# Seven stored left operands for the second token half, on a fused low-bit linear and gated MLP

## What is computed

```python
# x: (8, 256, 1024) f32; D = 1024, F = 2752
w   = dequantised(codebook, weight + 0.5 * lora_B @ lora_A) + 0.5 * lora_B @ lora_A
x1  = x + x @ w.T
g   = x1 @ W_gate.T + 0.5 * (x1 @ A_gate[i].T) @ B_gate[i].T     # i: adapter of the sample
u   = x1 @ W_up.T   + 0.5 * (x1 @ A_up[i].T)   @ B_up[i].T
a   = silu(g) * u
out = x1 + a @ W_down.T + 0.5 * (a @ A_down[i].T) @ B_down[i].T
```

## Time and profile before

| | us |
|---|---|
| median of 3 runs | 1620.17 (1619.71 to 1621.79) |
| the profiled execution's own time | 1620.05 |
| its span, first to last instruction | 1618.4 |
| TensorE busy in it | 1572.8 |
| VectorE busy | 1235.7 |
| ScalarE busy | 568.4 |
| GpSimd busy | 534.3 |
| mean granted TensorE clock | 0.993 |

### The profile page before, as it was taken

One profiled execution on the slowest core, in us unless ns is written; L12 is line 12 of the kernel. 1 busy time (PEld: TensorE's weight loads), 2 busy tenths in 40 slices (PEclk: granted clock), 3 DMA queues, 4 the chain that ended last, 5 costly groups with the idle time before them and its releaser, 6 DMA issues.

```text
span 1618.4 us, 21109 instructions
## 1 busy us (share of the span) xinstructions
PE 1572.8 (97%) x6968; PEld 1293.7 (80%) x6968; DVE 1235.7 (76%) x1575; ACT 568.4 (35%) x1006; POOL 534.3 (33%) x401
## 2 busy tenths in 40 slices
PE   6999999989999999996999999999999999999999
PEld 4888887868888878875888888888888888888887
DVE  6998969878888889987776888878675576785443
ACT  5411135433333333353433333333343233233231
POOL 4320013645555455653444555555410000000000
PEclk9999999999999999998999999999999999999999
DMA  9551174767887898881335666665267677586463
GB/s 287 126 115 64 63 227 107 194 176 218 213 217 196 218 234 221 238 309 51 99 122 137 175 182 180 183 179 155 83 198 209 163 184 191 148 222 206 157 188 119
DMA packets 368460, 281.25 MB, mean 174 GB/s; under 512 B 225120, under 2 KB 266848, under 8 KB 368224
## 3 DMA queue, kind: packets, MB, share of 16 engines
q1 hardware_dynamic: 284800, 245.11, 53.1%
q10 hardware_dynamic: 81472, 28.99, 7.1%
q0 software_dynamic: 2080, 5.80, 1.8%
HBM read 166.27 MB, written 110.85 MB: 171 GB/s over the span
## 4 chain that ended last, share of the span: by engine, by line
PE 81%; DVE 9%; SPq 3%; DMA 3%; issue 2%; ACT 1%; POOL 1%; DVEq 0%; ACTq 0%; POOLq 0%
PE bank L1826 18%; PE bankA L1826 12%; PE bankC L1826 12%; PE bank L2062 9%; PE bankC L2062 6%; PE bankA L2062 6%; PE bankT L1971 3%; PE bank L1971 3%; PE bankT L2062 3%; DVE xl L1337 2%; PE bankT L1877 1%; PE bankT L1878 1%; DVE rl L1328 1%; PE bankC L1842 1%; DMA WT_d<-wt 1%
## 5 line engine op out<-in xcount | busy, mean ns | idle before, releaser
L1023 ACT CAST rh<-wt 128x512 fp32r<-128x512 f32 x253 | 156.2, 620 | 363.9 <-PE bankC L1842 79.1
L1328 DVE TENSOR_TENSOR rl<-wt,rh 128x512 fp32r<-128x512 f32 x253 | 233.7, 931 | 21.7 <-ACT rh L1023 21.5
L1496 DVE TENSOR_TENSOR opl<-opl,oph 128x512 fp32r<-128x512 f32 (+1 forms) x154 | 107.6, 700 | 155.7 <-ACT oph L1139 155.4
L1826 PE MATMUL bank<-xh,rh 128*128 128x512 f32 x528 | 206.3, 391 | 3.1 <-issue 3.1
L1826 PE MATMUL bank<-xl,rh 128*128 128x512 f32 x528 | 206.0, 390 | 0.0
L1826 PE MATMUL bank<-xh,rl 128*128 128x512 f32 x528 | 206.0, 390 | 0.0
L1139 ACT CAST oph<-opl 128x512 fp32r<-128x512 f32 (+1 forms) x154 | 95.6, 621 | 268.4 <-DMA opl<-LT_d 260.5
L1826 PE MATMUL bankC<-xh,rh 128*128 128x512 f32 x352 | 138.8, 394 | 3.2 <-DVE xl L1337 1.9
L1826 PE MATMUL bankC<-xl,rh 128*128 128x512 f32 x352 | 138.5, 393 | 0.0
L1826 PE MATMUL bankC<-xh,rl 128*128 128x512 f32 x352 | 138.3, 393 | 0.0
L1826 PE MATMUL bankA<-xl,rh 128*128 128x512 f32 x352 | 137.1, 389 | 0.0
(11 more groups left out here) (209 smaller groups left out, 3664.9 us busy)
## 6 DMA issues: line engine op xcount, KB each, us to landing
opl<-LT_d SPq DMA_DIRECT2D x148, 256.0 KB, 2.9
WT_d<-wt SPq DMA_DIRECT2D x88, 256.0 KB, 3.2
RT_d<-dt SPq DMA_DIRECT2D x70, 256.0 KB, 3.2
opl<-RT_d SPq DMA_DIRECT2D x70, 256.0 KB, 3.8
LT_d<-ev ACTq DMA_DIRECT2D x60, 256.0 KB, 2.7
wb<-WT_d SPq DMA_DIRECT2D x44, 256.0 KB, 3.3
wt<-WT_d SPq DMA_DIRECT2D x44, 256.0 KB, 4.0
dn<-in_L_cond_W_down_dram SPq DMA_DIRECT2D x86, 128.0 KB, 3.9
```

The lines of the kernel that those rows point to most:

```text
L1023: nc.scalar.copy(rh[:, v % RING, 0:KH * rows], wsrc(mm, RSRC[p])).then_inc(s_hi, 1)
L1328: dv.tensor_tensor(rl[:, v % RING, 0:KH * rows], wsrc(mm, RSRC[p]), rh[:, v % RING, 0:KH * rows].bitcast(f32), ALU.subtract).then_inc(s_lo, 1)
L1496: dv.tensor_tensor(opl[0:rows, L_AT[n % NL], :], opl[0:rows, L_AT[n % NL], :].bitcast(f32), oph[0:rows, L_AT[n % NL], :].bitcast(f32), ALU ...
L1826: last = te.matmul(OUT[p], a[:, u % RING, cols], b[:, OPND[p], k, :], start=k == 0 and n == 0, stop=k == KH - 1 and n == 2 and (p in (0, 1 ...
```

## The change

- The first pass stores all seven forms of each block, once they are made (`store_form`, `FT_d`, 256 KB each), not the four quarters. The second pass loads them in pairs of 512 KB (`load_forms`, 77 loads) into ten slots `wq`, which lie over `wn` and `wt`, and GpSimd makes no weight sums in it.
- `w_s3` no longer waits for a store. `w_tr(mm, 0)` waits until five forms of the block before have landed (`s_fa`), `w_tr(mm, 3)` for the seventh, `w_s4` for the raw L12.
- The adapter rows A are summed once (`a_sums`, four GpSimd instructions) and patched into the seven forms of blocks 0 and 1 in 14 stores, spread over blocks 7 to 10.
- `act_sum` 3 writes `s1a` and not `ev`, so VectorE's `take` of an up block waits for the sum and not for its store. The sums, the down-adapter products `td` and their splits have other slots, above all in the two blocks after a change of row-group kind (`it` = 1, 12) and of pass (`it` = 11).
- `load_bn` and `load_an` move from SyncE's queue to ScalarE's. At the start, lora_A is SyncE's first load; lora_B and the first half of x come first on ScalarE's; VectorE splits lora_A ahead of the codebook arithmetic.

The forms, their stores and their loads:

```diff
-    WT_d = dram("WT_d", [2 * NJ, 4, P, KD // 2 * P], f32)
+    FT_d = dram("FT_d", [2 * NJ * 7, P, KD // 2 * P], f32)
-        wb = place("wb", [P, 4, KH * P], f32, S0 + 20480)
+        NQ = 10
+        wq = place("wq", [P, NQ, KH * P], f32, S0 + 20480)
+        def form(v):
+            return wt[:, RSRC[v % 7], :] if v < 7 * NH else wq[:, (v - 7 * NH) % NQ, :]
+        def form_ready(eng, v):
+            if v < 7 * NH:
+                s, n = ((s_tr, 1), (s_sum, 2), (s_tr, 4), (s_sum, 3), (s_sum, 1), (s_tr, 3), (s_sum, 4))[v % 7]
+                eng.wait_ge(s, 4 * (v // 7) + n)
             else:
+                pair = (v - 7 * NH) // 2
+                eng.wait_ge(s_wl[pair % len(s_wl)], 16 * (pair // len(s_wl) + 1))
...
+                def store_form(v):
+                    form_ready(sp, v)
+                    sp.dma_start(FT_d[v, :, :], form(v)).then_inc({2: s_f12, 6: s_f4}.get(v % 7, s_fa), 16)
+                def load_forms(pair):
+                    v = 2 * pair
+                    if pair == 0:
+                        sp.wait_ge(s_wal, 16 * 14)
                         sp.wait_ge(s_tr, 4 * NH)
...
+                    if pair == 2:
+                        sp.wait_ge(s_sum, 4 * NH)
+                        sp.wait_ge(s_fa, 80 * NH)
+                        sp.wait_ge(s_f12, 16 * NH)
+                        sp.wait_ge(s_f4, 16 * NH)
+                    if pair >= 2:
+                        sp.wait_ge(s_lo, 7 * NH + (-3, 0, -2)[pair - 2] if pair < 5 else 7 * NH + 2 * (pair - len(s_wl)) + 2)
+                    sp.dma_start(wq[:, v % NQ:v % NQ + 2, :], FT_d[v:v + 2, :, :].rearrange("k p n -> p k n")).then_inc(s_wl[pair % len(s_wl)], 16)
...
-                    if p in (1, 2, 3, 4) and mm + 1 < NH:
-                        store_wt(mm + 1, p - 1)
+                    if p == 1 and mm < NH:
+                        store_form(7 * mm + 6)
+                    for n in {1: (0,), 3: (5,), 4: (2, 4), 5: (1, 3)}.get(p, ()):
+                        if mm + 1 < NH:
+                            store_form(7 * (mm + 1) + n)
...
-                    if p == 5 and NH <= mm + 2 < NM:
-                        load_wt(mm + 2)
+                    for pair in range(7 * NH // 2):
+                        if u == 7 * NH + ((-11, -9, -6, -4, -6)[pair] if pair < 5 else 2 * pair - 11):
+                            load_forms(pair)
```

On GpSimd:

```diff
                     else:
-                        gp.wait_ge(s_al, 4 * it + 3)
-                        ins = tt(a12, a11, a12, ALU.subtract)
+                        gp.wait_ge(s_sst[0], 16 * (it + 1))
+                        ins = tt(s1a[r, :], a11, a12, ALU.subtract)
...
-                    turn = (5, 5, 7, 9) if first(it - 1) else (1, 1, 3, 7) if it == NJ else (1, 1, 3, 5)
-                    if p == 0 and 0 <= mm < NM:
+                    turn = (5, 5, 7, 7) if first(it - 1) else (4, 4, 6, 6) if it == NJ else (1, 1, 3, 4)
+                    if p == 0 and mm < NH:
                         w_s4(mm)
...
-                    if p == 2 and 0 <= mm + 1 < NM:
+                    if p == 2 and mm + 1 < NH:
                         w_s12(mm + 1)
```

On ScalarE:

```diff
+                    if (m, p) == (1, 6) and it != NJ - 1 and it + 2 < NIT:
+                        load_bn(it + 2)
+                    if (m, p) == (1, 6) and it != NJ - 1 and it + 1 < NIT:
+                        load_an(it + 1)
```

On VectorE:

```diff
-                    if n in (0, 2):
-                        wait(dve, s_wst[n], 16 * mm)
+                    if n == 0:
+                        wait(dve, s_fa, 80 * mm)
+                    if n == 3:
+                        wait(dve, s_f4, 16 * mm)
...
                         if m == 1:
                             wait(dve, s_a11, 16 * it)
-                            wait(dve, s_sst[3], 16 * it)
+                            wait(dve, s_as, 4 * it)
+                            wait(dve, s_al, 4 * it - 1)
...
-                    dve_tail(u, (6, 8, 10) if first(it - 1) else (4, 6, 9) if it == NJ else (1, 4, 7))
+                    dve_tail(u, (6, 8, 10) if first(it - 1) else (5, 9, 10) if it == NJ else (1, 4, 7))
```

On TensorE:

```diff
-                    td_at(u, (6, 8, 10, 12) if first(it - 1) else (2, 5, 8, 11) if it == NJ else (0, 3, 6, 9))
+                    td_at(u, (6, 8, 10, 12) if first(it - 1) else (3, 8, 10, 12) if it == NJ else (0, 3, 6, 9))
```

More of the change, by code:

```diff
@@ L393, in cond_resid_kernel @@
         s_wa = sem("p1_wa", st)
-        s_wst = [sem(f"p1_wst{i}", st) for i in range(4)]
-        s_wl = [sem(f"p1_wl{i}", st) for i in range(2)]
+        s_fa = sem("p1_fa", st)
+        s_f12 = sem("p1_f12", st)
+        s_f4 = sem("p1_f4", st)
+        s_wl = [sem(f"p1_wl{i}", st) for i in range(NQ // 2)]
         s_wat = sem("p1_wat", st)
@@ L514, in load_bn @@
-                def load_bn(it):
-                    h, j = it // NJ, jof(it)
-                    rows = rows_of(j)
-                    wait(sp, s_bt, 2 * it)
-                    for t in range(2):
-                        for g, src in enumerate((Bg_d, Bu_d)):
-                            q = 2 * t + g
-                            sp.dma_start(bn[q * Q:(q + 1) * Q, 0:2 * rows // Q, :],
-                                         src.rearrange("f b r -> f (b r)")[f_at(0, j):f_at(0, j) + 2 * rows, (2 * h + t) * CR:(2 * h + t + 1) * CR]
-                                         .rearrange("(a c) r -> c a r", c=Q)).then_inc(s_bn, 16)
@@ L605, in store_s @@
                     sp.dma_start(LT_d[(M5, M6, M3, M7)[n], h, j, 0:rows, :],
-                                 (s1a[:, :], s2a[:, :], s2a[:, :], ev[:, 1, 1, :])[n][0:rows, :]).then_inc(s_sst[n], 16)
+                                 (s1a, s2a, s2a, s1a)[n][0:rows, :]).then_inc(s_sst[n], 16)
                 def store_td(h):
@@ L677, in load_weight @@
                         sp.dma_start(lw[i * Q:(i + 1) * Q, :], weight[i * DI + o * Q:i * DI + (o + 1) * Q, :]).then_inc(s_lw, 16)
+                sp.dma_start(qsum[0:RL, :], lora_A).then_inc(s_la, 16)
                 sp.dma_start(cb[:, :], codebook.rearrange("(o n) -> o n", o=1).to_broadcast([P, LEVELS])).then_inc(s_cb, 16)
-                for i in range(NI):
-                    sp.dma_start(lb[i * Q:(i + 1) * Q, :, :],
-                                 lora_B[i * DI:i * DI + Q, None, :].to_broadcast([Q, 2, RL])).then_inc(s_lb0, 16)
-                sp.dma_start(qsum[0:RL, :], lora_A).then_inc(s_la, 16)
                 for i in range(NI):
@@ L774, in _ @@
                 store_bs(0, 1)
-                load_bn(1)
-                load_an(0)
                 def sums_at(it):
-                    return (6, 7, 8, 10) if first(it - 1) else (1, 2, 4, 8) if it == NJ else (1, 2, 4, 6)
+                    return (6, 7, 8, 9) if first(it - 1) else (5, 6, 7, 8) if it == NJ else (1, 2, 4, 5)
                 for u in range(END):
@@ L1006, in _ @@
                             dn_sums(rd, 3)
-                    if p == 4 and 0 <= mm + 1 < NM:
+                    if p == 4 and mm + 1 < NH:
                         w_s3(mm + 1)
@@ L1053, in load_wa, with load_bn, load_an @@
                                       .rearrange("(f c) d -> c f d", c=Q)).then_inc(s_wa, 16)
+                def load_bn(it):
+                    h, j = it // NJ, jof(it)
+                    rows = rows_of(j)
+                    wait(act, s_bt, 2 * it)
+                    for t in range(2):
+                        for g, src in enumerate((Bg_d, Bu_d)):
+                            q = 2 * t + g
+                            act.dma_start(bn[q * Q:(q + 1) * Q, 0:2 * rows // Q, :],
+                                         src.rearrange("f b r -> f (b r)")[f_at(0, j):f_at(0, j) + 2 * rows, (2 * h + t) * CR:(2 * h + t + 1) * CR]
+                                         .rearrange("(a c) r -> c a r", c=Q)).then_inc(s_bn, 16)
+                def load_an(it):
+                    h, j = it // NJ, jof(it)
+                    wait(act, s_ar, it)
+                    for half in range(2):
+                        for i in range(NI):
+                            i_ = min(i, rows_of(j) // Q - 1)
+                            act.dma_start(an[i * Q:(i + 1) * Q, half, :, :],
+                                         Ad_d[2 * h * CR:2 * (h + 1) * CR, f_at(half, j) + i_ * Q:f_at(half, j) + (i_ + 1) * Q]
+                                         .rearrange("(t c) r -> c t r", t=2)).then_inc(s_an, 16)
                 def b_hi(n):
@@ L1465, in dn_tr @@
                     wait(dve, s_dst[(0, 1, 3, 2)[b]], 16 * rd)
+                    if b == 0:
+                        wait(dve, s_ds, 4 * rd - 1)
                     if rd == 5:
@@ L1751, in _ @@
                             dn_tr(rd, B22)
[L1752 removed]
+                    if mm == NM // 2 + 1 and p == 6:
                         take_td(0)
```

179 lines of the change are left out of this document (77 added, 102 removed).

## The result

The changed kernel takes 1614.86 us, median of 7 runs (1613.19 to 1617.79), against 1620.17 (1618.46 to 1621.79, 7 runs): a ratio of 0.997, 95% interval 0.9959 to 0.9982. It is faster, but by 5.3 us and not by 20.5, and 0.9 us outside the range. The profiled execution took 1613.19 us with a span of 1611.5; it is the fastest of the seven.

What follows compares the result with a forecast made beforehand. TensorE, busy 97% of the span, was taken as the bound, so only its waits and low-clock time could be won. Terms -4 + 2.5 - 9 + 4 - 14 = -20.5 gave 1599.5 us, range 1588 to 1614.

Steps and rivals of the forecast that it cites:

- The start: Before block 0: lora_A loaded first lets TensorE's big matmuls start near 9.5; -4 us, bounds -2 and -4.5.
- Block 0: Twelve adapter loads on ScalarE delay the fifth operand's cast, partly hidden by lead: +2.5 us, between 0 and +5.
- Block 2: Third block of the first pass: the forecast gave it no term and no size of its own.
- in ordinary blocks: Sign of being wrong: VectorE standing at a transpose for an `FT_d` store in ordinary blocks; no size given.
- Blocks 3 and 4: `take` no longer waits for a store, and the low clock behind that wait goes: -9 us, at least -6.8.
- Blocks 5 to 21: Three more form stores per block load the DMA engines, against a freer SyncE queue: +4 us, between -2.7 and +15.
- The lower bound's reason: Blocks 5 to 21: SyncE's emptier queue removes even the losses of blocks 15, 17 and 19, -2.7 us.
- Blocks 22 and 23: Faster `x_lo` without GpSimd's sums, `td` moved to slot 8, loads next late: -14 us, between -9 and -18.8.
- Rival (b): Right operands' loads bound blocks 22 and 23, coming 9 us later than taken; gain 5, 1608.5 us; chance 0.11.
- Rival (c): W_down blocks of the first pass pay 2 us each, +15 in place of +4: 1610.5 us; chance 0.11.
- rival (e): No measurable change: W_down blocks' cost at 20 together with late right-operand loads in blocks 22 and 23; chance 0.05.
- at nothing: Rest of the second pass: 88 fewer GpSimd weight sums and shorter VectorE instructions gain nothing, TensorE being busy throughout.

Runs made afterwards that it cites:

- e11: The kernel before with only the change's order of the first loads: ratio 0.9974, 4.2 us off.
- e2: The changed kernel with load_bn(1) and load_an(0) moved on ScalarE's queue into block 0's slots 2 and 4: ratio 0.9949, 1610.7 us.
- e8: The changed kernel with ScalarE's early adapter loads moved into block 0's slots 2 and 4 and block 2's slots 1 and 4: ratio 0.9935, 1608.2 us.
- e16: The kernel before with new first-load order, fourth sum in s1a, later pair-11 slots, adapter loads on ScalarE placed in blocks 0 and 2, no forms: 1596.7 us.
- e10: The kernel before with only the fourth sum put into s1a and VectorE waiting for the sum, not its store: ratio 0.9947, 1610.9 us.
- e12: The kernel before, unchanged, profiled once more for scatter: 1620.2 us; its groups are six profiles without forms, eight with.
- e6: The changed kernel with three more form stores in each of blocks 5 to 21, written to a tensor nothing reads: ratio 1.0195, 1649.2 us.
- e5: The changed kernel with three steps of SyncE's queue reordered around block 22, same work: ratio 0.9951, 1611.9 us.
- e13: The kernel before with the new first-load order, fourth sum in s1a and later pair-11 slots, without stored forms: ratio 0.9874, 1598.4 us.

## Why the prediction was wrong

Its direction held, its size did not: of 20.5 us 5.3 came, 6.9 in the profile by which the steps are read. Step by step:

- **The start**, -4: measured -4.6 in the stretches, -4.2 alone (e11). The first large matmul runs at 9.09, forecast near 9.5. Right.
- **Block 0**, +2.5 between 0 and +5: measured +5.8, **over its bound**. The mechanism was right (ScalarE's issues between the casts; e2 takes them away and the block takes 23.1), the cover was not. I let "3 us of lead" hide part of it, but the fifth operand's cast, which came at 248.12, was needed at once: products 3 and 4, counted from 0, took 6.02 and 4.83 us where the kernel before has 2.72 for each, the second of them at a granted clock of 0.64.
- **Block 2**, not in the sum: measured **+6.3. This is the step that failed.** I counted the 12 issues that leave SyncE's queue once per pair as a gain there, and never asked what stands behind them on ScalarE at the end of block 1: the table load and the three `silu`. And I wrote that VectorE standing at a transpose for a store "in ordinary blocks" would prove me wrong; it did, in block 2, for 4.45 us. How the loss divides is open in part. Blocks 1 to 4 take 91.6 us in the changed kernel, 89.8 with the issues moved (e8), 86.8 with the issues moved and no forms (e16): the larger part, 3.0 against 1.8, is the forms and their stores.
- **Blocks 3 and 4**, -9: measured -8.4, and -8.6 alone (e10, 51.7 to 43.1). Right.
- **Blocks 5 to 21**, +4: measured +3.8 in the pair of profiles, 6.2 as a mean over many. Right in sign and size, but not in place, and so in part by luck. I put it into the W_down blocks and held blocks like 8 to be free of it. Of the 3.8, 3.0 lie in blocks 5 to 14 (211.5 against 208.5) and 0.8 in blocks 15 to 20 (128.7 against 127.9); the means of e12's two groups say 4.3 and 1.9. The DMA share is 0.91 in blocks 5 to 14, where I had under 0.85, and 0.92 in blocks 15 to 20, where I had about 1. And the sign that I had named came here too: in blocks 5 to 21 VectorE stood at a block's first transpose 11 times, 21.9 us in all and up to 3.2, where before it was 2.5 us in all and in e16 nothing. The profile puts these waits down to "issue" and not to a store; that only kernels with forms have them is what points at the stores. The lower bound's reason, an emptier SyncE queue, may be true for block 15 (e16); with the forms that block took anything from 20.9 to 23.2. By the HBM figure of the Trainium skill (DMA: Bandwidth & Descriptors, Specifications), about 358 GB/s, these blocks at 256 GB/s would have room and the term would be -2.7. The runs disagree: at 267 GB/s, far under that figure, the stretch of e6 had lost 35 us more.
- **Blocks 22 and 23**, -14: measured -9.9. Product 6 started 24.6 us after the block's start (742.88 - 718.30), where I took 735.5 - 715.28 = 20.2; that is the missing 4. I gave SyncE's stand for a landing 2 us; it was 5.5, behind it the second operand, and e5 wins 2.8 back by order alone. The gain's cause was half wrong: I put 6.5 us on GpSimd's sums leaving VectorE alone, and the last `x_lo` came 0.6 us earlier. One of the three slow ones remained, and e13 has the whole gain with the weight sums in place. The other half, `td` in a later slot, gave 8.6.
- Rival (b), the right operands' loads coming late, was near in mechanism, but it was the queue's order, not the loads' bytes, and it explains 3 of the 15 us that were missing. Rival (c) is nearest in time (1610.5), by luck: it puts +15 on blocks 5 to 21, which took 3.8 to 8.
- Two sums were wrong. The upper bounds of the start and of block 0 add 2 and 2.5 us to 1610.5, so 4.5 and not 3.5: by its own bounds the range should have ended at 1615, and 1614.86 would have lain in it, with the mechanisms as wrong as they are. And rival (e), "(c) at 20 and (b) together", makes 1624.5, 4.5 us slower than before, which is no "no change" by the 3.2 us taken there.

What I did not weigh at all is the change's balance. The forms, its largest part, cost 16.5 us with the moved issues that they need (e13 against the changed kernel, in medians): in the profiles 7.1 in block 0, 4.5 in blocks 1 and 2, 4.0 in blocks 5 to 21, and no gain in 22 and 23. Of the 16.5, 6.6 are ScalarE's issues in two bad places (e8). With the issues placed alike, the forms by themselves cost 11.5 us (e8, 1608.2, against e16, 1596.7; GpSimd's last sum of an ordinary pair comes one slot earlier in e8). The three small parts together give 20.8 us against the kernel before measured beside them (1619.1). What the forms were to save, GpSimd's sums in the second pass, lay beside a TensorE that was busy throughout; my own line "at nothing" said so.
